# Two boundaries and the output projection of a macaron block: when weights are loaded, how the last statistics are summed, how rows are centred and read back

## The chip, the cores and the metric

One Trainium2 chip, all 8 NeuronCores. Each core computes 1024 of the 8192 rows on its own; no core waits for another. The time is the device time in microseconds of the slowest core. The engines of a core are TensorE (PE), VectorE (DVE), ScalarE (ACT) and GpSimd (POOL); SyncE (SP) issues most DMAs, and POOL issues the stores. Each engine takes its instructions in the order in which they were emitted and waits on semaphores.

## The reference

```
x = x + 0.5 * ffn(layernorm(x))          # FFN 1
x = x + attn(layernorm(x))
x = x + 0.5 * ffn(layernorm(x))          # FFN 2, the same weights

ffn(x):  out = x @ W_base.T + b
         + 2 * sum over the top-2 of 8 experts, gate * B_e @ (A_e @ x), rank 16
attn(x): Q = x @ Wq.T (32 heads of 128), K, V = x @ Wk.T, x @ Wv.T (one head)
         rotary tables on Q and K
         windows of 512 keys every 256 rows, sigmoid(QK/sqrt(128)) / its row sum,
         neighbouring windows blended linearly; then @ Wo.T
layernorm: (x - mean) / sqrt(var + 1e-5), no weights
```

x is [2, 4096, 4096] fp32, the weights 4096 x 4096.

## The kernel before

Everything is transposed: features on the 128 partitions, rows of x along the free axis. A core holds 1024 own rows and 512 of its neighbours for K and V: three tiles t of 512 rows (t = 0 and 1 are its own, 2 the neighbours'). A tile of 4096 features is 32 chunks c of 128 x 512. The centred rows stand in SBUF as bf16 (`xc[t]`). A weight matrix is 32 tiles of 128 outputs, each 2 MB of fp32: two halves are loaded into two staging buffers and cast by ACT to bf16 into one of three slots (`wring`). One group (of, t) is 32 matmuls of 128x128 by 128x512 into one of four PSUM banks; in an FFN a 33rd adds the experts' part (`bpart`).

The stages, in the order in which every engine's program is written out by hand (there is no planner; `pr.emit` and `pr.dma` append to the lists of an engine, and the order of the Python calls is the order in each queue):

1. FFN 1 (lines 485 to 679): rows arrive, are centred, gated, and multiplied; x1 goes to HBM (`x1h`). From of = 3 to 28 the loop is of over t. The last three tiles 29 to 31 are done tile by tile in the order t = 2, 0, 1.
2. First boundary: the layernorm of x1. Its sums are kept by POOL in `acc1` and `acc2` (`evac`, lines 373 to 406), with the square by ACT. `bstats` (606) lets PE add them over the partitions, ACT and DVE make mean and variance. x1 is read back (`x1_load`) chunk by chunk into a ring of nine slots and centred by DVE (`bcenter`, 618). K and V of the three tiles (`kv_mm`, 719) follow chunk by chunk, with rotary tables (`tables`, 689, Sqrt on ACT and a reciprocal on DVE).
3. Attention, 64 slots of a head and half of the rows (lines 786 to 991).
4. Output projection (lines 993 to 1074, and 1103 to 1110): Wo on the heads' outputs, x1 read back and added by DVE (L389), sums by POOL, x2 to HBM (`x2h`).
5. Second boundary and FFN 2 (lines 1076 to 1202): x2 is read back into a ring of sixteen slots, centred, gated by `gating` (304), and multiplied; the first groups follow the centring chunk by chunk (`f2_k` with `chase`).

`wtile` (246) emits both loads and both casts of a weight tile at one place. In stage 4 that place is behind the groups of tile k, for tile k + 2:

```
tok = wo_group(of, t)                  # ends with wo_load(n + 4), an SP read of x1
wt_done[WT[of]]["end"] = tok
WT[of + 2] = wtile(wo_h[of + 2])       # SP: two loads; ACT: two casts
```

An evacuation reads its summand from one of four slots; the read for the fourth group on waits for the store, the add and the square of this one (`xs_free`).

## Time and profile before

| | us |
|---|---|
| median of three timed runs | 2874.55 (2871.07 to 2884.6) |
| the profiled execution | 2889.44 |
| its span on the slowest core (4) | 2887.7 |
| spans of the eight cores | 2854.6 to 2887.7 |
| PE busy | 2486.7 (86%) |
| DVE, ACT, POOL busy | 1095.7, 939.0, 753.9 |
| read from HBM, written | 408.65 MB, 58.72 MB |

A busy PE is not a PE at its peak: the granted clock of a stretch stands beside it. FFN 1 runs steadily from about 360 to 910 us, the first boundary to about 1094, attention to 1804, the output projection to about 2324, the second boundary to about 2480, FFN 2 to the end.

### The profile page before, as it was taken

The page shows a single profiled execution, that of the slowest core. Times are in us where ns is not written, and L with a number is a line of the kernel's source. Part 1 is how long each engine was busy: PE and PEld are TensorE (multiplying, and loading weights), DVE is VectorE, ACT ScalarE, POOL GpSimd, SP SyncE. Part 2 cuts the span into 40 slices and gives each one's busy share as a digit, 9 for nine tenths or more (in the row PEclk, how much of TensorE's full clock was granted, in tenths as well). Part 3 has the DMA queues.
Part 4 walks back from the last instruction along what each step waited for, and adds up shares of the span by engine and source line. Part 5 has one row for each costly group of instructions (what it writes and reads, how often), then busy time and mean ns, then how long its engine had stood idle before and what let it go on. Part 6 is the DMA issues. An engine that isn't in the chain of part 4 may idle for free.

```text
span 2887.7 us, 37498 instructions; the slowest of 8 cores (2854.6 to 2887.7 us)
## 1 busy us (share of the span) xinstructions
PE 2486.7 (86%) x12841; PEld 1198.4 (42%) x13084; DVE 1095.7 (38%) x2668; ACT 939.0 (33%) x1016; POOL 753.9 (26%) x696
## 2 busy tenths in 40 slices
PE   2645799999999868999999999978888788999999
PEld 2434344444443324444444444433333324444444
DVE  2334122211211667888888887100000034211111
ACT  2312122222222124555555554233322322122222
POOL 5645243444343201111111110423333330000000
PEclk9767899999999879999999999988999979999999
DMA  7521254445444883232232322455455575466664
GB/s 248 178 73 59 97 182 162 161 160 179 164 164 179 269 265 111 89 103 93 99 103 89 103 91 101 159 207 191 176 188 199 189 255 207 169 214 218 219 218 179
DMA packets 115307, 469.83 MB, mean 163 GB/s; under 512 B 14768, under 2 KB 15024, under 8 KB 79280
## 3 DMA queue, kind: packets, MB, share of 16 engines
q1 hardware_dynamic: 97200, 408.69, 41.6%
q0 software_dynamic: 17920, 58.73, 5.2%
q8 instruction: 106, 1.74, 0.3%
q14 instruction: 81, 0.66, 0.1%
HBM read 408.65 MB, written 58.72 MB: 162 GB/s over the span
## 4 chain that ended last, share of the span: by engine, by line
PE 40%; DMA 18%; DVE 16%; issue 9%; DVEq 8%; POOL 4%; ACT 3%; SPq 1%; ACTq 0%; POOLq 0%
PE PS L282 36%; DVEq L48 8%; DMA arena<-wo 7%; DMA x2h<-arena 4%; DMA arena<-wb 3%; DVE arena L891 3%; DVE arena L897 3%; POOL arena L439 3%; DMA arena<-x1h 2%; DVE arena L889 1%; DVE arena L893 1%; DVE arena L708 1%; SPq L43 1%; DVE arena L709 1%; DVE arena L621 1%
## 5 line engine op out<-in xcount | busy, mean ns | idle before, releaser
L282 PE MATMUL PS<-arena 128*128 128x512 bf16 x6953 | 1618.5, 390 | 121.3 <-ACT arena L239 106.9
L282 PEld LDWEIGHTS PS<-arena 128*128 128x128 bf16 x7102 | 707.4, 100 | 1004.5 <-issue 259.2
L239 ACT ACTIVATE arena<-arena 128x2048 bf16<-128x2048 f32 (+1 forms) x332 | 517.0, 1577 | 1108.3 <-DMA arena<-wb 644.3
L812 PE MATMUL PS<-arena 128*128 128x512 bf16 x1965 | 545.6, 380 | 4.4
L383 DVE TENSOR_TENSOR arena<-PS,arena 128x512 f32<-128x512 f32 x160 | 110.5, 690 | 890.8 <-PE PS L355 838.8
L854 ACT ACTIVATE arena<-PS 128x512 bf16<-128x512 f32 x384 | 229.0, 597 | 315.2 <-PE PS L851 312.0
L400 POOL TENSOR_TENSOR arena<-arena 128x512 f32<-128x512 f32 x160 | 207.4, 1296 | 429.6 <-ACT arena L398 424.6
L713 POOL TENSOR_TENSOR arena<-arena 128x512 bf16<-128x512 f32 x64 | 80.9, 1264 | 682.6 <-DVE arena L887 601.0
L812 PEld LDWEIGHTS PS<-arena 128*128 128x128 bf16 x2048 | 188.2, 98 | 138.6 <-issue 6.1
L389 DVE TENSOR_TENSOR arena<-PS,arena 128x512 f32<-128x512 f32 x64 | 44.1, 690 | 483.2 <-PE PS L282 478.0
L399 POOL TENSOR_TENSOR arena<-arena 128x512 f32<-128x512 f32 x160 | 215.7, 1348 | 3.4
L398 ACT ACTIVATE arena<-arena 128x512 f32<-128x512 f32 x160 | 95.5, 620 | 328.9 <-DVE arena L386 299.0
L870 PE MATMUL PS<-arena 128*128 128x130 bf16 x1536 | 130.7, 220 | 38.8 <-DVE arena L887 16.2
L43 POOL DMA_DIRECT2D out<-arena x64 | 34.6, 541 | 474.3 <-DVE arena L386 416.6
L870 PEld LDWEIGHTS PS<-arena 128*128 128x128 bf16 x1536 | 97.0, 97 | 142.7 <-issue 127.1
L851 PE MATMUL PS<-arena 128*128 128x512 bf16 (+1 forms) x512 | 145.7, 325 | 0.7
L386 DVE SCALAR_TENSOR_TENSOR arena<-arena 128x512 f32<-128x512 f32 x160 | 140.4, 878 | 15.5 <-issue 0.9
L43 POOL DMA_DIRECT2D x1h<-arena x96 | 53.7, 559 | 353.4 <-DVE arena L386 329.3
L621 DVE TENSOR_TENSOR arena<-arena 128x512 bf16<-128x512 f32 x160 | 113.3, 774 | 26.6 <-DMA arena<-x1h 23.5
L439 POOL TENSOR_TENSOR arena<-arena 128x512 f32<-128x512 f32 x72 | 115.1, 1598 | 11.0 <-POOL arena L439 0.9
L897 DVE SCALAR_TENSOR_TENSOR arena<-PS,arena 128x128 f32<-128x128 f32 x256 | 89.7, 350 | 24.9 <-issue 1.9
L891 DVE TENSOR_TENSOR arena<-arena 128x2 f32<-128x2 f32 x256 | 89.5, 350 | 25.1 <-issue 2.2
(95 smaller groups left out, 1237.2 us busy)
## 6 DMA issues: line engine op xcount, KB each, us to landing
arena<-wb SPq DMA_DIRECT2D x128, 1024.0 KB, 7.4
arena<-wq SPq DMA_DIRECT2D x64, 1024.0 KB, 5.0
arena<-wo SPq DMA_DIRECT2D x64, 1024.0 KB, 6.6
arena<-x1h SPq DMA_DIRECT2D x160, 256.0 KB, 5.1
arena<-x2h SPq DMA_DIRECT2D x128, 256.0 KB, 4.9
arena<-xp SPq DMA_DIRECT2D x12, 2048.0 KB, 11.8
arena<-xr SPq DMA_DIRECT2D x96, 256.0 KB, 2.7
x1h<-arena POOLq DMA_DIRECT2D x96, 256.0 KB, 2.4
```

Of the source, the lines that this page charges most:

```text
L48: self.ops[e].append((lambda v: v.drain(), (), None, 0))
L239: a.activation(d, s, ACT.Copy), [g, extra] if j == 0 else [])
L282: tok = pr.emit(PE, lambda t, c=c, b=b, w=w, n=n, fin=fin, r=rhs_t: t.matmul(bank(b), w[:, c, :], r[:, c, :], start=(n == 0), stop=(fin an ...
L399: p = pr.emit(POOL, lambda q: q.tensor_tensor(a1, a1, xs, ALU.add), [ev, acc_tok.get((f is f2, t))])
L400: q2 = pr.emit(POOL, lambda q: q.tensor_tensor(a2, a2, s, ALU.add), [sq])
L439: tok = pr.emit(POOL, lambda q, k=k: q.tensor_tensor(f_hs, f_hs, x[:, k * 512:(k + 1) * 512], ALU.add), [tok])
L812: tok = pr.emit(PE, lambda q, c=c: q.matmul(bank(b), w[:, c, :], xc[hf][:, c, :], start=(c == 0), stop=(c == NC - 1)), ws, c == NC - 1)
L851: tok = pr.emit(PE, lambda q, s=s, q0=q0, nq=nq, i=i: q.matmul(bank(b)[:, i * nq:(i + 1) * nq], krb[:, s * 128:(s + 1) * 128], qrb[u % 2][ ...
L854: sb_free[b] = sc_ev[(u, k)] = pr.emit(ACE, lambda a: a.activation(sgb[u % 2][:, k * 512:(k + 1) * 512], bank(b), ACT.Sigmoid, scale=SCALE ...
L870: tok = pr.emit(PE, lambda q, i=i, sl=sl, o=o: q.matmul(bank(b)[:, (i // 2) * 130:(i // 2) * 130 + 130], sgb[u % 2][:, o:o + 128], vext[:, ...
L891: pr.emit(DVE, lambda v: v.tensor_tensor(sm[:, 4:6], sm[:, 2:4], a01[:, 2 * Q:2 * Q + 2], ALU.mult))
L897: pr.emit(DVE, lambda v: v.scalar_tensor_tensor(t2, U[:, 130:258], sm[:, 6:7], t1, ALU.mult, ALU.add))
```

## The change

- **Loads and casts are separate.** `wload` issues the loads of a tile, `wcast` the two casts, which wait for the slot of the tile three before. In the steady loops tile of + 2 is cast at the start of tile of, and tile of + 3 is loaded right behind it.
- **Last statistics.** For the groups 29 to 31 of a row tile, ACT writes a bf16 copy and a bf16 square, and PE adds them over the partitions (`stat_mm`) at chunk 18 of a following group (10 and 18 for the last), on top of two fp32 matmuls over what POOL has summed up to tile 28. `stat_end` makes the mean and variance; the mean stays in PSUM.
- **Centring in pairs** of chunks, 128 x 1024: DVE reads the mean from PSUM, every fourth pair is POOL's, with the mean in SBUF.
- **Reads back.** Eight pairs of x1 are read at tile 25 of FFN 1 and the ring has eight slots (four at the end); twelve pairs of x2 are read at tile 26 of the projection, and eight more at the end of group (31, 0).
- **K and V of tile 2** use PSUM banks 0 and 1, and the order of the K/V block is changed. The tables use Ln and Exp on ACT.
- **Gating** is cut in three, which FFN 2 places apart: `rcolumn` (the four fp32 transposes of the row factor and their copy), `gating` (DVE and the sigmoids), `gtrans` (four transposes and a copy). An FFN evacuation writes its product back to PSUM and frees the bank after its second instruction.

The diff, cut to its core:

```diff
-    ring = [ring_r.again().f32(4608)[:, k * 512:(k + 1) * 512] for k in range(9)]
+    ring4 = [ring_r.again().f32(4096)[:, k * 1024:(k + 1) * 1024] for k in range(4)]
+    ring4 += [KVR.again().f32(4096)[:, k * 1024:(k + 1) * 1024] for k in range(4)]
...
-    def stage(src, dst, extra=None, parts=1):
+    stg_q = []
+
+    def load_half(src, dst, tile=None, hf=0):
+
         k = stg_n[0] % 2
         stg_n[0] += 1
-        g = pr.dma(SP, "stg%d" % k, stg[k], src, [stg_free[k]])
+        assert all(q[0] != k for q in stg_q)
+        stg_q.append((k, pr.dma(SP, "stg%d" % k, stg[k], src, [stg_free[k]]), dst, tile, hf))
+
+    def cast_half(extra=None, parts=1):
+        k, g, dst, tile, hf = stg_q.pop(0)
+        ws = [g, extra]
+        if tile is not None and tile >= 3 and hf == 0:
+            free = wt_done[tile - 3].get("end")
+            assert free is not None, tile
+            ws.append(free)
         s3 = resh(stg[k], (16, 128))
+        n = 16 // parts
         c = None
         for j in range(parts):
-            n = 16 // parts
             c = pr.emit(ACE, lambda a, d=dst[:, j * n:(j + 1) * n, :], s=s3[:, j * n:(j + 1) * n, :]:
-                        a.activation(d, s, ACT.Copy), [g, extra] if j == 0 else [])
+                        a.activation(d, s, ACT.Copy), ws if j == 0 else [])
         stg_free[k] = c
+        if tile is not None:
+            wt_done[tile]["tok"][hf] = c
         return c
...
-    def wtile(src, parts=1, half=None, k=None):
...
+    def wload(src, half=None, k=None):
...
         w = wring[k % 3]
-        free = wt_done[k - 3].get("end") if k >= 3 else None
-        if k >= 3:
-            assert free is not None, k
         for hf in ((0, 1) if half is None else (half,)):
-            wt_done[k]["tok"][hf] = stage(src[:, hf * 2048:(hf + 1) * 2048],
-                                          w[:, hf * 16:(hf + 1) * 16, :],
-                                          free if hf == 0 else None, parts)
+            load_half(src[:, hf * 2048:(hf + 1) * 2048], w[:, hf * 16:(hf + 1) * 16, :], k, hf)
+        return k
...
+    def wcast():
+
+        cast_half()
+        cast_half()
+
+    def wtile(src, parts=1, half=None, k=None):
+        k = wload(src, half, k)
+        for _ in ((0, 1) if half is None else (half,)):
+            cast_half(None, parts)
...
         if kind == "ffn":
-            tm = f["tmp"][j]
-            e = pr.emit(DVE, lambda v: v.tensor_tensor(
-                tm, bank(b), f["rh"][:, t * 512:(t + 1) * 512], ALU.mult), [mm, xs_ld[n]])
+            pr.emit(DVE, lambda v: v.tensor_tensor(
+                bank(b), bank(b), f["rh"][:, t * 512:(t + 1) * 512], ALU.mult), [mm, xs_ld[n]])
             pr.drain()
             ev = pr.emit(DVE, lambda v: v.scalar_tensor_tensor(
-                xs, tm, bh[:, of:of + 1], xs, ALU.add, ALU.add))
+                xs, bank(b), bh[:, of:of + 1], xs, ALU.add, ALU.add))
         else:
-            e = ev = pr.emit(DVE, lambda v: v.tensor_tensor(xs, bank(b), xs, ALU.add), [mm, xs_ld[n]])
-        bank_free[b] = e
+            ev = pr.emit(DVE, lambda v: v.tensor_tensor(xs, bank(b), xs, ALU.add), [mm, xs_ld[n]])
+        bank_free[b] = ev
         st = pr.dma(POOL, "st%d" % k, dst, xs, [ev])
         st_tok[(kind, of, t)] = st
         free = [st]
-        if stat:
+        s = f["sqs"][j]
+        if stat == "late":
+            sb = s.bitcast(BF16)
+            pr.emit(ACE, lambda a: a.activation(sb[:, 0:512], xs, ACT.Copy), [ev, sqs_free[j]])
+            sq = pr.emit(ACE, lambda a: a.activation(sb[:, 512:1024], xs, ACT.Square))
+            late.setdefault((kind, t), []).append((sb, sq, j))
+            free.append(sq)
+        elif stat:
             a1 = f["acc1"][:, t * 512:(t + 1) * 512]
             a2 = f["acc2"][:, t * 512:(t + 1) * 512]
-            s = f["sqs"][j]
             sq = pr.emit(ACE, lambda a: a.activation(s, xs, ACT.Square), [ev, sqs_free[j]])
-            p = pr.emit(POOL, lambda q: q.tensor_tensor(a1, a1, xs, ALU.add), [ev, acc_tok.get((f is f2, t))])
+            p = pr.emit(POOL, lambda q: q.tensor_tensor(a1, a1, xs, ALU.add), [ev, acc_tok.get((kind, t))])
             q2 = pr.emit(POOL, lambda q: q.tensor_tensor(a2, a2, s, ALU.add), [sq])
-            acc_tok[(f is f2, t)] = q2
+            acc_tok[(kind, t)] = q2
             sqs_free[j] = q2
-            acc_tok[t] = q2
             free += [p, sq]
         xs_free[k] = free
         return ev
+
+    late = {}
...
+    def stat_mm(f, kind, t, n, bm_, bs_, ws=()):
+
+        if n == 0:
+            for src, b in ((f["acc1"], bm_), (f["acc2"], bs_)):
+                pr.emit(PE, lambda q, b=b, s_=src[:, t * 512:(t + 1) * 512]: q.matmul(
+                    bank(b), onesf, s_, start=True, stop=False), [acc_tok[(kind, t)]] + list(ws), False)
+        sb, sq, j = late[(kind, t)][n]
+        pr.emit(PE, lambda q: q.matmul(bank(bm_), onesb, sb[:, 0:512], start=False, stop=(n == 2)), [sq], False)
+        tok = pr.emit(PE, lambda q: q.matmul(bank(bs_), onesb, sb[:, 512:1024], start=False, stop=(n == 2)))
+        sqs_free[j] = tok
+        return tok
+
+    def stat_end(f, t, bm_, bs_, tok):
+
+        a1 = f["acc1"][:, t * 512:(t + 1) * 512]
+        a2 = f["acc2"][:, t * 512:(t + 1) * 512]
+        pr.emit(ACE, lambda a: a.activation(a1, bank(bm_), ACT.Copy), [tok])
+        m = pr.emit(ACE, lambda a: a.activation(a2, bank(bm_), ACT.Square))
+        v = pr.emit(DVE, lambda v: v.tensor_tensor(a2, bank(bs_), a2, ALU.subtract), [m])
+        return m, v
 
 
...
+    def pair_load(key, src, t, c, slot, slot_key, waits):
+        rg_ld[key] = pr.dma(SP, "rg%s" % slot_key, slot, src[t, c:c + 2].rearrange("c p n -> p c n"),
+                            [rg_free.get(slot_key)] + list(waits))
+
+    def pair_center(f, key, t, c, slot, slot_key, dst, bm_, m_tok, pe_tok, eng):
+        o = dst[:, c:c + 2, :]
+        if eng == DVE:
+            mean = bank(bm_)
+        else:
+            mean = f["acc1"][:, t * 512:(t + 1) * 512]
+        rg_free[slot_key] = pr.emit(eng, lambda v: v.tensor_tensor(
+            o, slot, mean.unsqueeze(1).broadcast_to([128, 2, 512]), ALU.subtract),
+            [rg_ld[key], m_tok, pe_tok])
+        return rg_free[slot_key]
...
+    def x1_center(k):
+        for _ in range(k):
+            n = x1_done[0]
             t, c = x1_seq[n]
-            ctr2[(t, c)] = bcenter(f1, t, c, n, ring, xc[t], bm[t], xdone[t])
-            x1_load(1)
-
-    for t in (2,):
-        for of in range(29, 32):
+            sk, sl = x1_slot(n)
+            ctr2[(t, c)] = ctr2[(t, c + 1)] = pair_center(
+                f1, n, t, c, sl, sk, xc[t], MB[t][0], bm[t], xdone[t], POOL if n % 4 == 3 else DVE)
+            x1_done[0] += 1
+            while x1_n[0] < len(x1_seq) and x1_n[0] - (8 if x1_n[0] < 36 else 4) <= n:
+                x1_load(1)
...
+    W[3] = wtile(wb_h[3])
+    W[4] = wtile(wb_h[4])
+    W[5] = wload(wb_h[5])
+    for of in range(3, 29):
+        wcast()
+        if of + 3 < 32:
+            W[of + 3] = wload(wb_h[of + 3])
+        for t in range(3):
             tok = f1_k(of, t)
...
+    wcast()
+    Wk = wload(wk_h)
+    g, tok, mm = f1_last(29, 2)
+    f1_lev(29, 2, g, mm)
+    g, tok, mm = f1_last(30, 2, at(18, lambda: f1_late(2, 0, stat_ws)))
+    f1_lev(30, 2, g, mm)
+    g, tok, mm = f1_last(31, 2, at(18, lambda: f1_late(2, 1)))
+    f1_lev(31, 2, g, mm)
+    xdone[2] = tok
+
+    g, tok, mm = f1_last(29, 0, at(18, lambda: f1_late(2, 2)))
+    stat_done(2, box["tok"])
+    x1_center(2)
+    f1_lev(29, 0, g, mm)
+    g, tok, mm = f1_last(30, 0, at(18, lambda: f1_late(0, 0, stat_ws)))
+    x1_center(5)
+    f1_lev(30, 0, g, mm)
+    g, tok, mm = f1_last(31, 0, at(18, lambda: f1_late(0, 1)))
+    x1_center(5)
+    f1_lev(31, 0, g, mm)
...
-    Wk = Wv = None
...
+    g, tok, mm = f1_last(29, 1, at(18, lambda: f1_late(0, 2)))
+    wt_done[W[29]]["end"] = tok
+    x1_center(4)
+    c2_end = [pr.now(DVE)]
+    stat_done(0, box["tok"])
+    f1_lev(29, 1, g, mm)
+    wcast()
+    Wv = wload(wv_h)
+    g, tok, mm = f1_last(30, 1)
+    wt_done[W[30]]["end"] = tok
+    x1_center(5)
+    f1_lev(30, 1, g, mm)
+    wcast()
+    WQ = {0: wload(wq_h[0])}
+    g, tok, mm = f1_last(31, 1, at(18, lambda: f1_late(1, 0, c2_end)))
+    wt_done[W[31]]["end"] = tok
+    x1_center(5)
+    f1_lev(31, 1, g, mm)
+    wcast()
...
-        r2_tok[t] = pr.emit(DVE, lambda v: v.reciprocal(a2, a2), [s])
-        pr.drain()
+        ln = pr.emit(ACE, lambda a: a.activation(a2, a2, ACT.Ln, bias=eps1, scale=1.0), [bv[t]])
+        r2_tok[t] = pr.emit(ACE, lambda a: a.activation(a2, a2, ACT.Exp, scale=-0.5), [ln])
         dst = tabh if t == 2 else tab[t]
...
-    kv_mm(2, 0)
-    bm[1], bv[1] = bstats(f1, 1)
+    WQ[1] = wload(wq_h[1])
...
+    kv_mm(2, 0, late1)
+    late_end = box["tok"]
+    x1_center(3)
+    stat_done(1, late_end)
     tb2 = tables(2, 0)
-    x1_center(64, 74)
+    x1_center(3)
+    ctr0_end = pr.now(DVE)
+    kvr_ws = [rg_free[k] for k in range(4, 8)]
+    kv_mm(2, 1)
     k_evac(2, tb2)
-    kv_mm(2, 1)
+    bank_free[0] = kv_free[0]
+    x1_center(4)
+    kv_mm(0, 0)
     v_evac(2)
+    bank_free[1] = kv_free[1]
+    x1_center(3)
     tb0 = tables(0, 1)
-    x1_center(74, 85)
-    kv_mm(0, 0)
+    kv_mm(0, 1)
     v_trans(2)
     k_evac(0, tb0)
-    kv_mm(0, 1)
+    x1_center(4)
     v_evac(0)
-    x1_center(85, 96)
+    x1_center(5)
...
+    wcast()
+    WT[3] = wload(wo_h[3])
...
+            pair_load(n, x2h, t, c, sl, "x%d" % sk, [st_tok[("wo", c, t)], st_tok[("wo", c + 1, t)]] +
+                      (att_ws if n < 12 else [o0_done]))
...
+            if n >= 8:
+                ws += [rg_free["x%d" % k] for k in range(4)]
+            if n >= 16:
+                ws += [rg_free["x%d" % k] for k in range(4, 12)]
+            eng = POOL if n % 4 == 3 else DVE
+            o = xc3[t][:, c:c + 2, :]
+            mean = bank(MB2[t][0]) if eng == DVE else f2["acc1"][:, t * 512:(t + 1) * 512]
+            ctr3[(t, c)] = ctr3[(t, c + 1)] = rg_free["x%d" % sk] = pr.emit(
+                eng, lambda v, o=o, sl=sl, mean=mean: v.tensor_tensor(
+                    o, sl, mean.unsqueeze(1).broadcast_to([128, 2, 512]), ALU.subtract),
+                [rg_ld[n], bm2[t]] + ws)
+            x2_done[0] += 1
+            while 20 <= x2_n[0] < len(x2_seq) and x2_n[0] - 8 <= n:
+                x2_load(1)
...
+        if of > 1:
+            wcast()
+            if of not in (4, 5):
+                if of + 3 < 32:
+                    WT[of + 3] = wload(wo_h[of + 3])
+        if of == 4:
...
+            load_half(wa_h[:, 0:2048], f2["ar"][:, 0:16, 0:128])
+            load_half(wa_h[:, 2048:4096], f2["ar"][:, 16:32, 0:128])
...
+            if of in (4, 5) and t == 0:
+                cast_half()
+                bb2_tok = cast_half()
+                WT[of + 3] = wload(wo_h[of + 3])
+        if of == 4:
+            ar2_tok = bb2_tok
+        if of == 26:
+            x2_load(12)
         wt_done[WT[of]]["end"] = tok
-        if of + 2 < 32:
-            WT[of + 2] = wtile(wo_h[of + 2])
...
+    g, mm = wo_last(29, 0)
+    wo_lev(29, 0, g, mm)
+    g, mm = wo_last(30, 0, at(18, lambda: f2_late(0, 0, b2_ws)))
+    wo_lev(30, 0, g, mm)
+    g, mm = wo_last(31, 0, at(18, lambda: f2_late(0, 1)))
+    wo_lev(31, 0, g, mm)
+    o0_done = mm
+    x2_load(8)
+
+    g, mm = wo_last(29, 1, at(18, lambda: f2_late(0, 2)))
+    wt_done[WT[29]]["end"] = mm
+    stat2_done(0, box["tok"])
+    x2_center(3)
+    wo_lev(29, 1, g, mm)
+    wcast()
+    WF[1] = wload(wb_h[1])
+    g, mm = wo_last(30, 1, at(18, lambda: f2_late(1, 0, b2_ws)))
+    wt_done[WT[30]]["end"] = mm
+    x2_center(5)
+    wo_lev(30, 1, g, mm)
+    wcast()
+    WF[2] = wload(wb_h[2])
+    g, mm = wo_last(31, 1, at(18, lambda: f2_late(1, 1)))
+    wt_done[WT[31]]["end"] = mm
+    x2_center(5)
+    wo_lev(31, 1, g, mm)
+    wcast()
+    WF[3] = wload(wb_h[3])
...
+        ln = pr.emit(ACE, lambda a: a.activation(rh, a2, ACT.Ln, bias=eps4, scale=4.0), [bv2[t]])
+        rh_tok[t] = pr.emit(ACE, lambda a: a.activation(rh, rh, ACT.Exp, scale=-0.5), [ln])
+        return rh_tok[t]
...
-    f2_k(0, 0, True)
-    bm2[1], bv2[1] = bstats(f2, 1)
-    rchain2(0)
-    x2_center(32, 42)
+    f2_k(0, 0, True, at(18, lambda: f2_late(1, 2)))
+    stat2_done(1, box["tok"])
+    r0 = rchain2(0)
+    x2_center(3)
+    ar_free[0], ar_free[1] = bv2[0], bv2[1]
+    for p in range(4):
+        at_ = aphase_piece(f2, xc3[0], p, [ar2_tok])
     f2_k(1, 0)
-    for p in range(4):
-        at = aphase_piece(f2, xc3[0], p, [ar2_tok])
-    hw2[0] = None
-    x2_center(42, 50)
+    rc2 = rcolumn(f2, 0, r0, None)
+    b6_free[0] = rc2
+    g2 = gating(f2, 0, at_, rc2)
+    x2_center(6)
     f2_k(2, 0)
-    hw2[0] = gating(f2, 0, at, rchain_tok[0], b6_free[0])
-    b6_free[0] = pr.now(ACE)
-    rchain2(1)
-    x2_center(50, 64)
+    hw2[0] = gtrans(f2, 0, g2)
+    r1 = rchain2(1)
+    x2_center(7)
     wt_done[WF[0]]["end"] = f2_k(0, 1, True)
-    WF[3] = wtile(wb_h[3])
+    wcast()
+    WF[4] = wload(wb_h[4])
     for _ in range(3):
         f2_b()
+    for p in range(4):
+        at_ = aphase_piece(f2, xc3[1], p, [])
+    rc2 = rcolumn(f2, 1, r1, b6_free[0])
+    g2 = gating(f2, 1, at_, rc2)
     wt_done[WF[1]]["end"] = f2_k(1, 1)
-    WF[4] = wtile(wb_h[4])
-    for p in range(4):
-        at = aphase_piece(f2, xc3[1], p, [])
+    wcast()
+    WF[5] = wload(wb_h[5])
     wt_done[WF[2]]["end"] = f2_k(2, 1)
-    hw2[1] = gating(f2, 1, at, rchain_tok[1], b6_free[0])
-    first3 = f2_k(3, 0)
+    hw2[1] = gtrans(f2, 1, g2)
+    f2_k(3, 0)
     pend2.insert(0, pend2.pop())
-    f2_b()
...
     for of in range(3, 32):
+        if of > 3:
+            if of + 2 < 32:
+                wcast()
+            if of + 3 < 32:
+                WF[of + 3] = wload(wb_h[of + 3])
```

## Rows read from the trace of the kernel before

**Rows 1.** Waits of PE over the span: total us, times, longest.
```profile
PE PS L282 <- ACT arena L239: 106.9, 30, 20.7
PE PS L610 <- POOL arena L400: 26.5, 2, 15.1
PE PS L757 <- DVE arena L748: 18.9, 2, 9.6
PE PS L1151 <- DVE arena L621: 17.0, 23, 5.1
```

**Rows 2.** Busy time by stretch: PE, PEld, DVE, ACT, POOL, clock, DMA, GB/s.
```profile
1804.30:2323.90 519.60, 440.22 (x1856) 190.96 (x1891) 42.89 (x62) 154.50 (x126) 182.51 (x180) 0.92 0.52 186
2480.00:2882.00 402.00, 395.20 (x1790) 178.02 (x1825) 79.33 (x110) 103.15 (x54) 29.93 (x56) 1.00 0.61 213
909.80:1094.40 184.60, 131.92 (x537) 57.38 (x547) 111.09 (x148) 37.57 (x34) 31.94 (x31) 0.84 0.77 255
2323.90:2480.00 156.10, 123.46 (x662) 59.18 (x670) 69.58 (x118) 32.36 (x32) 22.25 (x20) 0.85 0.64 213
```

**Rows 3.** Timeline of DVE in the output projection: start, us, instruction [idle before].
```profile
2161.70 0.69 DVE L389 TENSOR_TENSOR arena<-PS,arena 128x512 f32<-128x512 f32 x1 [6.88 <-PE PS L282]
2168.61 0.69 DVE L389 TENSOR_TENSOR arena<-PS,arena 128x512 f32<-128x512 f32 x1 [6.21 <-PE PS L282]
```

**Rows 4.** Waits of the SP queue in the output projection.
```profile
SPq L1216 <- DMA x2h<-arena: 269.8, 51, 21.2
SPq L1216 <- ACT arena L398: 161.2, 28, 9.9
```

**Rows 5.** Timeline of all engines in the output projection.
```profile
2057.74 5.72 SPq L43 DMA_DIRECT2D arena<-x1h  x2
...
2063.51 0.92 SPq L43 DMA_DIRECT2D arena<-wo  x2
...
2068.91 1.91 ACT L239 ACTIVATE arena<-arena 128x2048 bf16<-128x2048 f32 x1 [10.73 <-DMA arena<-wo]
...
2071.08 14.17 PE L282 MATMUL PS<-arena 128*128 128x512 bf16 x57 [2.83 <-ACT arena L239]
```

**Rows 6.** DMA issues of the page: KB each, median us to landing.
```profile
arena<-wb SPq DMA_DIRECT2D x128, 1024.0 KB, 7.4
```

**Rows 7.** Busy time by stretch, first boundary.
```profile
990.00:1000.00 10.00, 9.91 (x39) 4.17 (x39) 6.14 (x10) 2.78 (x2) 0.56 (x1) 0.82 1.00 346
...
1020.00:1030.00 10.00, 5.79 (x11) 2.15 (x12) 7.62 (x9) 1.13 (x2) 3.51 (x3) 0.52 0.99 319
```

**Rows 8.** Busy time of FFN 1, of core 0 and then of core 4.
```profile
400.00:900.00 500.00, 494.18 (x2290) 223.85 (x2288) 101.02 (x140) 129.63 (x116) 216.13 (x210) 1.00 0.49 174
400.00:900.00 500.00, 497.09 (x2190) 222.63 (x2233) 101.45 (x136) 123.29 (x112) 208.77 (x203) 0.96 0.46 167
```

**Rows 9.** Timeline of PE at the first boundary.
```profile
910.04 7.07 PE L282 MATMUL PS<-arena 128*128 128x512 bf16 x31
...
946.91 1.02 PE L610 MATMUL PS<-arena 128*128 128x512 f32 x2
...
948.63 7.07 PE L282 MATMUL PS<-arena 128*128 128x512 bf16 x32
...
981.60 2.04 PE L610 MATMUL PS<-arena 128*128 128x512 f32 x2 [11.44 <-POOL arena L400]
...
1024.21 2.04 PE L610 MATMUL PS<-arena 128*128 128x512 f32 x2 [15.07 <-POOL arena L400]
```

**Rows 10.** Instructions of two lines: duration in ns, min/median/max.
```profile
L459 DVE TENSOR_TENSOR arena<-arena x12: 4410/4426/5492, 42.3 to 265.2; 128x4096 bf16<-128x4096 f32 x12
L399 POOL TENSOR_TENSOR arena<-arena x160: 1272/1277/6627, 162.5 to 2368.0; 128x512 f32<-128x512 f32 x160
```

**Rows 11.** Timeline of PE: second boundary (A phase), and the end.
```profile
2351.69 2.28 PE L1151 MATMUL PS<-arena 128*128 128x512 bf16 x4 [5.12 <-DVE arena L621]
...
2436.94 7.74 PE L297 MATMUL PS<-arena 128*128 128x136 bf16 x128
...
2881.87 0.38 PE L355 MATMUL PS<-arena 128*128 128x512 bf16 x1
```

264 lines of the change are left out of this document (124 added, 140 removed).

## The prediction, made before the changed kernel was run

> **What bounds the kernel now.** I read in this order: who waited for whom over the whole span, the busy time by stage, then the timeline of each stage that loses time. TensorE (PE) is the bound, and its work doesn't change much, so the question is where it stands still and where it runs at the lower clock. In the list of waits five eighths of what this change can reach is one line: 106.9 us, in 30 waits, for the cast of a weight tile (L282 on L239); then come 26.5 us for the statistics' adds (L610 on POOL's L400), 18.9 us for the V evacuation and 17.0 us for centring [rows 1]. By stage, PE was busy 440.2 of 519.6 us in the output projection (D, to the end of group (31,0)), 131.9 of 184.6 us at the first boundary (B, from the start of group (29,2) to the second Q group), 123.5 of 156.1 us at the second (E), at granted clocks of 0.92, 0.84 and 0.85; in the steady second FFN it is 395.2 of 402.0 us at 1.00 [rows 2]. Attention and the first 900 us are not touched in any way that PE sees.
>
> The price of full speed: two evacuations in D lie 6.91 us apart, that is 32 matmuls of 0.216 us [rows 3]. A group of 33 in an FFN costs 7.13 us.
>
> **Why D waits.** SP issues in order. The read of x1 for the evacuation four groups on waits for the store that frees its slot (SP waited 269.8 us for stores and 161.2 us for the squares) [rows 4], and the weights of tile k+2 are queued behind it. In the timeline the two reads hold SP from 2057.74 to 2063.46, the weights go out at 2063.51, the cast can start at 2068.91, and PE goes on at 2071.08 after 2.83 us [rows 5]. The cast at the head of ACT's queue also holds back the squares, so POOL's adds and the next store, which feeds the first delay.
>
> **D, part by part.** After: tile k+3 is loaded once tile k+2 is cast, and cast one tile later. The load leaves SP some 5.5 us into a tile (same SP delay), lands 7.4 us later (median of the wb loads [rows 6]), at 13 to 15; its cast is due at 13.8 + 1.5, and PE wants it 12 us after that. So the waits of 75 us in this window and the slow matmuls behind them go. Sum: 59 groups x 6.91 = 407.7; last head 0.4; statistics of tile 0, two fp32 matmuls as now 1.7 and four bf16 ones 0.9 (the last two lie in E); 410.7 in all, against 519.6. Added: twelve reads of 0.5 MB after tile 26, 6.3 MB. At the 319 GB/s of a full DMA [rows 7] they take 20 us and stand ahead of tile 30's weights; the slack is about 27 us, so 0 to 8, I take 4. The staging of A and B at tiles 4 and 5 delays a load by a tile at most, out of two tiles of slack: 0 to 4, I take 0. Clock: a dense FFN 1 ran at 1.00 on core 0 and 0.96 on core 4 for 500 us [rows 8]; on 411 us this is 0 to 17, I take 6. D = 421, saves **99** (bounds 80 to 109).
>
> **B.** Now: 910.04 to 1094.38. PE stands from 970.16 to 981.60 and from 1009.14 to 1024.21 because the square and adds of the last group come late, behind casts and eleven centrings; the chases behind crawl [rows 9]. After, at full speed: 521 matmuls of 0.216 = 112.5; three statistics of 1.72 (bank 6 and 7 fp32 matmuls, 946.91 to 948.63 [rows 9]) + 6 x 0.216 = 9.1; transposes 1: 122.6. It can't be reached, for two reasons.
> (1) DMA. Only 8 of 48 pairs are preloaded. From the first centring, which needs the mean of tile 2 at chunk 18 of (29,0), 31.5 us into B, 40 pairs (21.0 MB), three weight tiles (6.3 MB) and some 3.2 MB of reads, stores and tables must pass: 30.5 MB at 319 GB/s = 96 us, so the last pair lands at about 127, where PE at full speed would need it at 114. After it: its centring 1, the rest of kv_mm(1,0) about 1, kv_mm(1,1) 6.9.
> (2) The end of B stays serial on VectorE (DVE): tables, rope, V evacuation, transposes. The reciprocal on DVE goes, the ACT pair that replaces it is behind the cast of WQ[1]: I take 6 of the wait, now 18.9 - 9.6 = 9.3 [rows 1] (bounds 2 to 10).
> Sum 127 + 2 + 6.9 + 6 = 142; restarts at half clock 2: 144, saves **40** (bounds 15 to 58; full DMA reached 346 in one stretch [rows 7], and the in-order ACT may cost more: the cast of WQ[0] stands ahead of stat_done(1)).
> Centring: a DVE pair is 1024 elements. 4096 took 4.41 us [rows 10], so 1.08 ns each and about 1.17 us for a pair with its start. Pairing itself gives next to nothing, since the cost goes with the elements; the fourth pair on POOL does: 1.28 us for 512 [rows 10], so 2.5. Bounds for the DVE pair with a PSUM mean, which the trace doesn't show: 1.1 to 1.4 (a PSUM and an SBUF input took 0.69 for 512, isolated [rows 3]). None of it is on the path while DMA is.
>
> **E.** Now: 2323.9 to the last matmul at 2882.25 [rows 11], 558.4. Full speed: three groups 20.7, statistics 3.5, 64 FFN groups x 33 x 0.216 = 456.2, two A phases x 7.7 [rows 11], gating on PE 3: 498.9. Loss now 59.4, of which the two crawling chases, two gatings (PE waits for L339) and the evacuation behind them. After, with T the start of (29,1): the mean of tile 0 is there at T+6; DVE does 12 pairs and three evacuations, POOL four; pair 15 is ready at about T+26 where PE wants it at T+30. No wait. For tile 1 ACT must first cast WF[2], which lands at T+30, so the mean comes at T+33, not T+29; pairs 16 to 18 follow, then DVE is held by the gating until T+51 and the rest is done at T+64 where the chase begun at T+54 would end at T+61: 4 lost. The burst of four evacuations holds bank 3: 2.6 (now 1.8), as an evacuation keeps its bank for both of its instructions, 1.5 us in place of 0.7. In the steady FFN this is hidden by four banks of 7.1 us each. DMA 2, clock 3. E = 510.5, saves **48** (bounds 30 to 58).
>
> The rest: Ln and Exp in place of Sqrt and reciprocal are beside PE; FFN 1's evacuation through PSUM is hidden (DVE was busy 79.3 of 402.0 us in a steady FFN [rows 2]); the 20.7 us wait for W[3], the longest of its line [rows 1], stays, because SP still reaches W[3] after the same reads: 0. W[5] is now cast ahead of the squares of the first groups: POOL gets late by some 10 us and has 20.
>
> Total 99 + 40 + 48 = 187. The profiled execution took 2889.4 us with its span of 2887.7, above all the three timed runs (median 2874.55): core 4's 0.96 in FFN 1 is about 20 us of it, which no edit touches. So I take 187 off the median: **2687.5**.
>
> **A rule weighed.** POOL's add beside DVE's back-to-back centrings took up to 6.63 us, 1.28 otherwise [rows 10]. The Trainium skill (page "SBUF — State Buffer", section on the engine and DMA sides) says that a DVE instruction with two SBUF inputs takes a port pair that GpSimd shares and keeps it to its end; with the mean in PSUM there is one SBUF input, and by that rule POOL's pair stays at 2.5. No row shows POOL beside a run of centrings with a PSUM mean, so this is open until the profile after.
>
> **Rivals.**
> (a) The boundaries give little: DMA is full for B, ACT's casts stand before both second means. B saves 15, E 25, D 99: 2874.5 - 139 = **2736**. For: DMA share 0.99 at 1020 [rows 7]; against: E's volume fits.
> (b) Dense work lowers the clock. D and E get 0.96 as core 4 did: 0.04 x 909 = 36, less the 9 that I have: 2687 + 27 = **2714**. Against: the second FFN at 1.00 with PE 98% busy. The Trainium skill (page "TensorE: Matmul & The Clock Gate", section "Seeing it yourself") says more: a peak-current limiter takes a die with three densely working cores to 13/16. By that the 909 us would become 1119 and the gain would be gone (about 2897); rows 2 and 8 show 402 and 500 us of dense work without it, on a die whose cores all work.
> (c) Slower than before: POOL's pairs. 20 of the 80 pairs go to POOL, and each is waited for in order by DVE's slots and by PE. If DVE starves POOL as it does now, a pair costs up to 2 x 6.63 = 13.3, 265 in all on the path: 2687 + 265 = **2952**. It decides from 187/20 = 9.4 us a pair. Against: the rule above, and that a starved POOL holds only 12 + 8 spots.
> (d) The change doesn't do what it says in D: not the order of SP but DMA volume is the limit (3.1 MB per 13.8 us = 227 GB/s, in bursts). Then D saves 50: **2737**. Against: the steady FFN moves 213 GB/s at a share of 0.61 without waits [rows 2].
>
> **How the numbers follow.** Forecast 0.62 (own range 2662 to 2712), (a) 0.18, (b) 0.08, (d) 0.08, (c) and the limiter together 0.03, something within half a per cent of no change 0.01. Half a per cent (14 us) is what this measurement tells from none. The range takes in (a), (b) and (d) and the low bound of all three parts (109 + 58 + 58 = 225 gives 2650): 2655 to 2748. Faster 0.96, same 0.01, slower 0.03.
>
> **What would show it.** D: waits of L282 for the cast near 0, PE about 99% busy, evacuations 6.9 apart throughout. B: DMA share near 1 from the first centring to kv_mm(1,0), PE waits only there and before the V transposes, 144 long. E: no wait before the first FFN group, a few us in the chase of tile 1. POOL's pairs at 2.5 us. Wrong if the D waits stay with loads landing late, if the clock of dense stretches is under 0.95 on most cores, or if B is longer than 170.

## The result, and the profile after

2713.4 us (median of 4 runs, 2710.7 to 2725.3) against 2879.6 for the kernel before, measured beside it (4 runs, 2871.1 to 2889.8): a ratio of 0.943, 95% interval 0.938 to 0.948. It is 6% faster; 166 us went, where 187 were forecast. The forecast was 2687.5; 2713.4 lies just above its own range (2662 to 2712) and inside the whole range (2655 to 2748). In some executions of every kernel the cores of one die show a lower granted clock and the time is some per cent longer; the ratios and times below leave those out. The profiled execution took 2725.3 us (span 2723.4), 164.1 less than the one before (2889.4).

Stages of the profiled executions, slowest core, in us (in brackets the median over the eight cores):

| stage | before | after | saved | forecast |
|---|---|---|---|---|
| A, to the start of group (29,2) | 910.0 (891.9) | 898.6 (882.6) | 11.4 (9.3) | 0 |
| B, first boundary | 184.3 (183.8) | 177.1 (173.8) | 7.2 (10.0) | 40 |
| C, attention | 709.9 (710.2) | 711.2 (711.0) | -1.3 (-0.8) | 0 |
| D, projection to (31,0) | 519.6 (513.8) | 421.4 (420.2) | 98.2 (93.6) | 99 |
| E, to the last matmul | 558.3 (558.8) | 509.6 (511.5) | 48.7 (47.3) | 48 |

D and E came as forecast. B gave a fifth to a quarter of its forecast, and A gave 9 to 11 us that I had put at nothing. The total is nearer to its forecast than B is only because A, by luck, paid back a third of what B lacked.

Waits of PE over the span, after (total, times, longest), to be laid beside [rows 1]:

```profile
PE PS L831 <- DVE arena L657: 26.9, 4, 13.8
PE PS L306 <- ACT arena L251: 23.7, 2, 22.0
...
PE PS L450 <- ACT arena L426: 16.0, 3, 9.3
```

The 106.9 us for the cast of a weight tile are 23.7, and 22.0 of them are W[3]'s in FFN 1, which the prediction left standing. The adds' 26.5 us became 16.0 for the copies and squares that PE now sums (L450 on L426). The line at the top is centring in the K/V block (L657), for which PE did not wait in the kernel before.

The windows that answer to [rows 2], in the order B, D, E, steady FFN (length, busy time of PE, PEld, DVE, ACT, POOL, granted clock, DMA share, GB/s):

```profile
898.60:1075.67 177.07, 131.51 (x553) 56.36 (x563) 76.00 (x85) 39.79 (x44) 36.46 (x24) 0.86 0.68 218
1786.80:2208.20 421.40, 411.47 (x1863) 186.41 (x1900) 43.11 (x62) 152.10 (x126) 178.19 (x176) 0.99 0.71 247
2208.20:2717.90 509.70, 498.13 (x2456) 235.12 (x2500) 128.43 (x186) 137.68 (x92) 55.10 (x75) 1.00 0.62 217
2300.00:2700.00 400.00, 395.37 (x1808) 180.05 (x1843) 83.82 (x116) 103.08 (x55) 31.34 (x58) 1.00 0.61 215
```

D went from a clock of 0.92 to 0.99. In B the DMA share *fell*, from 0.77 to 0.68, where I had it near 1.

**D after.** One tile of the timeline of all engines, against [rows 5]:

```profile
2057.75 32.54 PE L306 MATMUL PS<-arena 128*128 128x512 bf16 x147
...
2065.08 3.69 ACT L251 ACTIVATE arena<-arena 128x2048 bf16<-128x2048 f32 x2
...
2066.65 1.54 SPq L43 DMA_DIRECT2D arena<-x1h  x2
...
2068.28 0.90 SPq L43 DMA_DIRECT2D arena<-wo  x2
...
2078.89 3.69 ACT L251 ACTIVATE arena<-arena 128x2048 bf16<-128x2048 f32 x2
```

The weights asked for at 2068.28 are cast at 2078.89 without a wait, and a tile takes 13.81 us (2065.08 to 2078.89), 64 matmuls at full speed.

**B after.** Timelines of PE, of DVE, and of SP's queue:

```profile
984.88 0.58 PE L450 MATMUL PS<-arena 128*128 128x512 bf16 x1 [9.27 <-ACT arena L426]
...
1016.47 9.98 PE L831 MATMUL PS<-arena 128*128 128x512 bf16 x37 [13.77 <-DVE arena L657]
...
1047.32 4.13 PE L831 MATMUL PS<-arena 128*128 128x512 bf16 x8 [10.29 <-DVE arena L657]
```

```profile
979.46 2.53 DVE L657 TENSOR_TENSOR arena<-arena,PS 128x1024 bf16<-128x1024 f32 x2 [8.65 <-DMA arena<-x1h]
981.90 0.69 DVE L411 TENSOR_TENSOR PS<-PS,arena 128x512 f32<-128x512 f32 x1
...
1012.66 1.68 DVE L800 TENSOR_TENSOR arena<-arena 128x512 f32<-128x512 f32 x1 [15.46 <-DMA arena<-sinx]
...
1055.92 1.22 DVE L657 TENSOR_TENSOR arena<-arena,PS 128x1024 bf16<-128x1024 f32 x1 [0.80 <-DMA arena<-x1h]
```

```profile
991.98 3.87 SPq L43 DMA_DIRECT2D arena<-wq  x2
...
998.02 0.70 SPq L43 DMA_DIRECT2D arena<-sinx  x1
1021.48 10.70 SPq L43 DMA_DIRECT2D arena<-x1h  x7
```

These rows form a circle. The rotary tables (cos, sin) are asked for behind 2 MB of Q weights; DVE stands 15.46 us for them, with centrings behind it whose data are there; a centring that isn't done frees no slot, so SP asks for no x1 from 997 to 1021.48; and the DMAs then run dry. Windows of after (DMA share and GB/s at the end of the row):

```profile
1000.00:1010.00 10.00, 2.70 (x13) 1.02 (x11) 0.00 (x0) 0.49 (x1) 0.87 (x1) 0.79 1.00 344
1010.00:1020.00 10.00, 3.42 (x9) 1.06 (x10) 7.03 (x8) 0.00 (x0) 2.34 (x1) 0.53 0.13 49
...
1040.00:1050.00 10.00, 2.45 (x6) 0.45 (x7) 9.68 (x12) 0.00 (x0) 2.59 (x1) 0.50 0.07 10
```

**E after.** The longest waits of PE from 2208 on:

```profile
PE PS L306 <- DVE arena L414: 2.7, 1, 2.7
PE PS L321 <- DVE arena L461: 2.5, 1, 2.5
PE PS L1335 <- POOL arena L1203: 1.8, 1, 1.8
PE PS L1335 <- DVE arena L1203: 1.6, 3, 0.7
```

### The profile page after: what moved, and what is told of

Read it like the earlier page. It is cut to its first block, busy times and chain, and to the rows that moved or that the text cites. A ratio compares the mean times of both kernels' runs of the same rounds, so it can differ in the third digit from the quotient of the medians.

```text
span 2723.4 us, 37240 instructions; the slowest of 8 cores (2698.8 to 2723.4 us)
## 1 busy us (share of the span) xinstructions
PE 2436.5 (89%) x12871; PEld 1191.4 (44%) x13114; DVE 1024.1 (38%) x2563; ACT 946.4 (35%) x1036; POOL 755.4 (28%) x686
## 4 chain that ended last, share of the span: by engine, by line
PE 57%; DVE 15%; DVEq 8%; DMA 6%; issue 6%; POOL 3%; ACT 2%; SPq 1%; another core or an unknown queue 0%; POOLq 0%; ACTq 0%
PE PS L306 53%; DVEq L48 8%; DVE arena L1008 3%; DVE arena L1014 3%; POOL arena L495 2%; DVE arena L1006 2%; DMA arena<-wb 2%; DVE arena L809 2%; DVE arena L1010 1%; DVE arena L810 1%; PE PS L384 1%; DMA arena<-wo 1%; SPq L43 1%; ACT arena L523 1%; DMA arena<-sinx 1%
## 5 line engine op out<-in xcount | busy, mean ns | idle before, releaser
L306 PE MATMUL PS<-arena 128*128 128x512 bf16 x6956 | 1579.1, 384 | 35.5 <-ACT arena L251 23.7
L251 ACT ACTIVATE arena<-arena 128x2048 bf16<-128x2048 f32 (+1 forms) x332 | 510.1, 1572 | 508.5 <-PE PS L306 229.6
L929 PE MATMUL PS<-arena 128*128 128x512 bf16 x1964 | 545.3, 380 | 3.3
L411 DVE TENSOR_TENSOR PS<-PS,arena 128x512 f32<-128x512 f32 x160 | 111.8, 699 | 892.6 <-PE PS L384 828.7
L434 POOL TENSOR_TENSOR arena<-arena 128x512 f32<-128x512 f32 x145 | 184.5, 1273 | 50.8 <-ACT arena L432 50.8
L433 POOL TENSOR_TENSOR arena<-arena 128x512 f32<-128x512 f32 x145 | 192.7, 1329 | 3.1
L417 DVE TENSOR_TENSOR arena<-PS,arena 128x512 f32<-128x512 f32 x64 | 44.2, 691 | 383.4 <-PE PS L306 351.7
L968 PE MATMUL PS<-arena 128*128 128x512 bf16 x511 | 145.5, 326 | 1.9
L414 DVE SCALAR_TENSOR_TENSOR arena<-PS,arena 128x512 f32<-128x512 f32 x160 | 120.1, 750 | 15.6 <-issue 0.9
L495 POOL TENSOR_TENSOR arena<-arena 128x512 f32<-128x512 f32 x72 | 114.5, 1591 | 11.0 <-POOL arena L495 0.9
L43 POOL DMA_DIRECT2D x2h<-arena x64 | 35.7, 557 | 233.0 <-DVE arena L417 232.9
## 6 DMA issues: line engine op xcount, KB each, us to landing
arena<-x1h SPq DMA_DIRECT2D x48, 512.0 KB, 8.6
```

Source lines behind the costliest of these rows:

```text
L43: self.ops[e].append((lambda q, o=out, i=in_: q.dma_start(out=o, in_=i), tuple(t for t in waits if t is not None), sem, 16))
L251: a.activation(d, s, ACT.Copy), ws if j == 0 else [])
L306: tok = pr.emit(PE, lambda t, c=c, b=b, w=w, n=n, fin=fin, r=rhs_t: t.matmul(bank(b), w[:, c, :], r[:, c, :], start=(n == 0), stop=(fin an ...
L433: p = pr.emit(POOL, lambda q: q.tensor_tensor(a1, a1, xs, ALU.add), [ev, acc_tok.get((kind, t))])
L434: q2 = pr.emit(POOL, lambda q: q.tensor_tensor(a2, a2, s, ALU.add), [sq])
L495: tok = pr.emit(POOL, lambda q, k=k: q.tensor_tensor(f_hs, f_hs, x[:, k * 512:(k + 1) * 512], ALU.add), [tok])
```

## The experiments

Ratios are to the kernel before, measured beside each. Stage lengths are medians over the eight cores of the profiled run, against the brackets in the table above; kernels are named after what they change.

**a_old_place**: the kernel after, with the projection's weights where they were.

```diff
-        if of > 1:
-            wcast()
-            if of not in (4, 5):
-                if of + 3 < 32:
-                    WT[of + 3] = wload(wo_h[of + 3])
...
         wt_done[WT[of]]["end"] = tok
+        WT[of + 2] = wtile(wo_h[of + 2])
```

> The changed kernel with one part undone: the weight tiles of the output projection are loaded and cast at the old place, behind the groups of tile k for tile k+2. Theory 1 (the place of the loads in SP's queue made the waits, and moving it gave the 98 us of D): D goes back from 421 to about 515 us, PE waits for casts of about 75 us come back, the whole is 2713 + 94 = about 2805. Rival (the gain in D came from elsewhere, e.g. from the staging of A and B or the early reads): D stays under 450 and the whole under 2745.

Ratio 0.986 (0.977 to 0.996), 2839.2 and 2840.5 us where 2805 were expected; D 534.2 (after: 420.2; expected 515), B 172.7, E 510.2. PE waits 111.8 us for the cast, as before. The weights' edit is the whole gain of D. That D is 20 us longer than before's 513.8 comes from the twelve early reads of x2, which this kernel keeps: SP asks for them at 2232.97, ahead of two reads of the next weights, and here nothing is loaded ahead to cover it. ACT's cast waits, and PE then stands 19.3 us at 2260.64, where before has no wait over 11.0 in D.

```profile
2258.48 1.91 ACT L251 ACTIVATE arena<-arena 128x2048 bf16<-128x2048 f32 x1 [30.84 <-DMA arena<-wo]
```

**b_head**: the kernel before, with load and cast of tile k+2 at the head of tile k.

```diff
+        if of > 1:
+            WT[of + 2] = wtile(wo_h[of + 2])
         tok = None
...
-        if of + 2 < 32:
-            WT[of + 2] = wtile(wo_h[of + 2])
```

> The kernel before with one thing moved: the loads and casts of weight tile k+2 of the projection are emitted ahead of the groups of tile k instead of behind them. No third tile ahead. Theory 1 (place in SP's queue): the loads leave some 14 us earlier, D falls from 520 to 420 to 440 us and the whole from about 2878 to 2790. Rival (two tiles ahead are not enough, since a cast at the head of ACT's queue waits for its load and holds the squares, the adds, the stores and so SP): half the waits stay, D about 470, the whole about 2830.

Ratio 0.995 (0.993 to 0.997); D 501.6, 12 of after's 94 us, and longer than either theory had (420 to 440, or 470). A place one tile further forward in SP's queue, which the prediction named first, is worth little. The timeline of all engines shows why:

```profile
2070.23 5.76 SPq L43 DMA_DIRECT2D arena<-x1h  x2
...
2076.04 0.94 SPq L43 DMA_DIRECT2D arena<-wo  x2
...
2081.20 1.91 ACT L239 ACTIVATE arena<-arena 128x2048 bf16<-128x2048 f32 x1 [10.52 <-DMA arena<-wo]
...
2083.89 1.91 ACT L239 ACTIVATE arena<-arena 128x2048 bf16<-128x2048 f32 x1 [0.78 <-DMA arena<-wo]
2085.70 1.13 ACT L398 ACTIVATE arena<-arena 128x512 f32<-128x512 f32 x2
2086.39 5.83 SPq L43 DMA_DIRECT2D arena<-x1h  x2
```

A closed loop of 16.16 us (2070.23 to 2086.39) against the 13.8 that PE needs: two reads (5.8), weights asked for, landed and cast by 2085.80 (9.8), the square that had waited at the cast's back (0.57), and only then is the slot free for the next read.

**l_no_sums**: the kernel before; the sums of x2 and of its squares are left out in the projection, so nothing stands behind a cast.

```diff
-        evac(f2, "wo", of, t, g, mm, x2h[t, of])
+        evac(f2, "wo", of, t, g, mm, x2h[t, of], stat=False)
```

> The kernel before with the sums of x2 left out in the output projection (no square on ACT, no two adds on POOL), the weights at their old place. Theory 4 (a closed loop through ACT: a cast waits for its load at the head of ACT's queue, the squares wait behind it, the adds and the next store behind them, SP's reads behind those, the next weights behind the reads; one turn takes 16 us where two groups take 13.8): with the squares gone the loop is open, D falls from 520 to 420 to 435, PE's waits for casts from 75 to under 10 us. Theory 1 as first put (the weights are simply issued too late, behind the reads of their own tile): store 4 + reads 6 + landing 7 + cast 2 = 19 us from the last evacuation is still over 13.8, D stays above 480.

Ratio 0.970 (0.966 to 0.974); D 434.1 (expected 420 to 435), 80 us shorter with the weights at their old place. Opening the loop is enough. What is left to 420 are waits for the cast of 22.5 us in 15 on one core, more than the 10 expected. The edit takes the squares and POOL's adds out together, so it doesn't say which of them weighs more; in b_head's rows it is the square that lets the next read go.

**q_cast_now**: the kernel after; in tiles 9 to 27 the weights are asked for directly ahead of their cast, not a tile earlier.

```diff
-        if of > 1:
+        if 9 <= of <= 27:
+            WT[of + 2] = wload(wo_h[of + 2])
             wcast()
...
+        elif of > 1:
+            wcast()
```

> The kernel after, with one thing changed in 19 tiles of the output projection (9 to 27): the tile's weights are asked for directly ahead of their cast (both at the head of the tile two ahead of their use), where the change asks for them a whole tile before the cast. Theory (the cast and the squares share ScalarE, so a cast whose transfer is under way holds the squares, the squares hold the adds, the adds the store and the buffer, and these the next reads): the 19 tiles go at a period of 15.5 to 16.5 us where the kernel after has 13.9 to 14.1, so the projection stage is 30 to 45 us longer (451 to 465 for 420.2), and the whole 2740 to 2758. Rival (what counts is only that the reads are issued at the head of the tile): the stage stays within 5 us of 420, the whole within 0.2% of the kernel after.

Ratio 0.962 (0.959 to 0.965); D 470.5. From tile to tile SP's weight reads lie 16.4 us apart (1882.41 to 2161.31 in 17 steps), the upper end of what I expected. D is longer than the 451 to 465 expected, since at the hand-over behind tile 27 one more wait of 21.7 us came up: as in a_old_place, the twelve early reads of x2 (2176.61) stand ahead of the next weights, and no tile is loaded ahead to cover it. With b_head and l_no_sums this settles D: what counts is that the transfer lies *between* the request and the cast, in time in which ACT works.

**c_halfread**: the kernel after; of each x1 pair at the first boundary only one half is read, and used twice.

```diff
-            pair_load(n, x1h, t, c, sl, sk, [st_tok[("ffn", c, t)], st_tok[("ffn", c + 1, t)]] + rg_ws)
+            rg_ld[n] = pr.dma(SP, "rg%s" % sk, sl[:, 0, :], x1h[t, c],
+                              [rg_free.get(sk), st_tok[("ffn", c, t)], st_tok[("ffn", c + 1, t)]] + rg_ws)
```

> The changed kernel with half of x1's read back left out at the first boundary: each pair reads only its first chunk, which is centred twice, so 12.6 MB of 25.2 MB go. All instructions and their order stay. B was 177 us where 144 was forecast. Theory 2 (volume: DMA full is what B waits for): B falls by up to 10.5 MB / 319 GB/s = 33 us, to about 145. Theory 3 (order: DVE stands at the tables' multiplications for cos and sin, which are queued behind the Q weights, and no x1 read is issued meanwhile): the wait before the tables shrinks only as far as the queue ahead of cos and sin does, the gaps with an idle DMA stay, and B falls by 15 us at most, to 162 or more.

Ratio 0.938 (0.932 to 0.944); B 150.9, 23 less, between the two theories (145, and 162 or more). So volume counts; but a third less of it leaves B still above the 144 forecast with all of it. It isn't volume alone either: the shorter queue ahead of the tables cuts DVE's two waits for sin from 15.46 and 7.96 us to 9.61 and 5.39.

**d_wq1_late**: the kernel after, Q's second weight tile asked for behind the second pair of tables.

```diff
-    WQ[1] = wload(wq_h[1])
...
     tb0 = tables(0, 1)
+    WQ[1] = wload(wq_h[1])
```

> The changed kernel with the load of the second Q weight tile (2.1 MB) issued behind the loads of cos and sin of both tables instead of ahead of them. Theory 3 (order): cos and sin land 6 to 7 us earlier, DVE's wait at the first tables falls from 15.5 to about 9 and that at the second from 8 to about 8 (nothing was moved there), B about 168, whole about 2705. Theory 2 (volume): the same bytes still pass before the last pair, so B stays at 174 to 178 and the wait only moves.

Ratio 0.943 (0.934 to 0.953), the same as after's: the whole time, expected at 2705, doesn't show it (median 2716.1, 2701.2 to 2730.9). The stage does: B 165.5, 8 less for one moved line, with every byte still ahead of the last reads of x1, and DVE's first wait for sin is 8.40 us (expected 9).

**e_order**: the kernel after, the whole first boundary reordered: both pairs of tables are asked for ahead of the K/V block, Q's weights behind its first centrings, and centrings go ahead of tables and K evacuation.

```diff
+    tload(2, 0)
+    tload(0, 1)
...
     stat_done(1, late_end)
+    WQ = {0: wload(wq_h[0])}
...
+    x1_center(4)
     tb2 = tables(2, 0)
...
     tb0 = tables(0, 1)
+    wcast()
+    WQ[1] = wload(wq_h[1])
```

> The changed kernel with the first boundary reordered: cos and sin of two tables are issued ahead of both Q weight tiles; the first Q tile is loaded at the start of the K/V block and cast behind the tables' Ln and Exp, the second is loaded behind that cast; on DVE the evacuation of (31,1) stands ahead of the last two of its five centrings, and the first tables' multiplications stand behind four more centrings. The halved read took 27 us off B and the later load of one tile 12, so both volume and order count. If it is the order of the queues (theory 3): the 9.3 us wait for the late copy, the 15.5 us wait for sin and the idle DMA at 1010 and 1040 go, B falls from 177 to 140 to 150, whole about 2685. If volume alone (theory 2): DMA passes the same 30 MB from the first centring to the last pair, but moves 4 MB of it behind the last x1 pair, so at most 13 us: B 164, as with the one tile moved.

2692.8 us (2692.1 to 2699.6), ratio 0.934 (0.930 to 0.938); B 155.6, 18 less, which again lies between the theories (140 to 150, and 164; their 27 and 12 us are of the slowest core). Two windows, 119 to 139 us into B (after's 0.13 lies at 111 to 121):

```profile
1000.00:1010.00 10.00, 5.54 (x20) 1.55 (x18) 7.63 (x11) 0.00 (x0) 0.00 (x0) 0.82 0.99 293
1010.00:1020.00 10.00, 3.73 (x8) 0.84 (x8) 3.73 (x4) 0.00 (x0) 3.17 (x2) 0.50 0.83 294
```

The DMAs no longer run dry before the last pair is in, and its centring begins 134.9 us into B (DVE, 1016.3) where after has 157.3 (1055.92). Contrary to theory 2, both Q tiles are still asked for ahead of the last reads of x1 (997.37 and 999.73): from the first centring to that one the core moved 289 GB/s over 104.4 us at a share of 0.91, 30.2 MB. The bytes are the same; the rate rose.

**r_best**: e_order, with the casts behind the copies and squares that PE waits for, at both boundaries.

```diff
     f1_lev(31, 1, g, mm)
+    wcast()
...
     wo_lev(29, 0, g, mm)
+    wcast()
+    WF = {0: wload(wb_h[0])}
...
     r0 = rchain2(0)
+    wcast()
+    WF[3] = wload(wb_h[3])
```

> The kernel of e_order (first boundary reordered, 2692.8), with the casts on ScalarE put behind the copies and squares that TensorE waits for, at both boundaries: the second half of the V weights behind the late copy of (31,1), the last projection weights behind (29,0)'s, the third FFN tile's behind (31,1)'s, and that of the fourth behind the statistics. In e_order TensorE waits 5.7 us, 8.1 us (two times) and 4.0 us for ScalarE at these places (core 0). Theory: they go, and 2/3 of them isn't lost again to the transfers behind: first boundary 151 to 154 (155.6 before), last stage 502 to 507 (512.0), projection within 3 of 421.9: whole 2678 to 2688. Rival (these waits only stand in for transfers that arrive too late, so that the wait moves to a centring or to weights): within 0.15% of e_order's 2692.8.

Profiled at 2677.8 us, the shortest execution of all; median 2684.8 (2677.8 to 2706.6), ratio 0.936 (0.932 to 0.940), which overlaps e_order's: that it beats e_order isn't settled by the times. By stage it does: B 154.2 (e_order 155.6), D 412.1 (421.9), E 509.9 (512.0). The gain isn't where it was expected: E was to be 502 to 507, and D within 3 us of 421.9. What is left in B, waits of PE from 860 to 1060:

```profile
PE PS L867 <- DVE arena L858: 13.0, 2, 7.2
PE PS L838 <- POOL arena L657: 10.5, 3, 6.2
```

**i_no_early_x2**: the kernel after, the twelve early pairs of x2 asked for with the others behind (31,0).

```diff
-        if of == 26:
-            x2_load(12)
...
-    x2_load(8)
+    x2_load(20)
```

> The kernel after, with the first 12 pairs of the second boundary's read-back asked for behind group (31,0) with the next 8, in place of behind tile 26. Theory: in the projection nothing is gained (the DMAs have room, within 1.5 us), and at the boundary the 12 pairs (6.3 MB at some 320 GB/s, 20 us) come one after the other in front of TensorE's chase, which the last three groups (21 us) cover only in part: the last stage is 12 to 25 us longer (524 to 537 for 511.5), whole 2725 to 2738. Rival (the chase is paced by the centrings on VectorE, 38 pairs in 45 us, not by the transfers): the last stage stays within 4 us of 511.5.

Ratio 0.946 (0.943 to 0.948). E 527.0, 15.5 longer, the size expected but not for the reason: the chase waits 3.1 us in all (after 3.4), and the loss is one wait for the copies behind a cast.

```profile
2225.99 0.58 PE L450 MATMUL PS<-arena 128*128 128x512 bf16 x1 [17.91 <-ACT arena L426]
```

The FFN's weights are now asked for behind twenty pairs of x2 (SP, from 2177.27; the weights at 2204.49), ACT's cast stands 21.54 us for them, and the copy stands behind the cast: the knot of D once more. And D is 410.3, 10 *shorter*, which neither theory had. Reading x2 early is worth some 6 us, not 16: it holds up the last projection weights, and the copies that stand behind their cast (L450 on L426, 6.2 us in after's D, not there here).

**g_all_dve** and **h_mean_sbuf**: the kernel after, with all 80 pairs on DVE; and with DVE's pairs reading the mean from SBUF (the `if False` leaves the copy for both engines).

```diff
-            eng = POOL if n % 4 == 3 else DVE
+            eng = DVE
```

```diff
-        if eng == DVE:
+        if False:
             mean = bank(bm_)
...
-            mean = bank(MB2[t][0]) if eng == DVE else f2["acc1"][:, t * 512:(t + 1) * 512]
+            mean = f2["acc1"][:, t * 512:(t + 1) * 512]
```

> The changed kernel with all 80 pairs centred by DVE, none by POOL. DVE gets 12 + 8 more pairs of 1.2 us. At the first boundary DMA is what centring waits for, so B stays within 4 us of 177. At the second, tile 1 has four more DVE pairs between the gating and the chase: E from 510 to 515, at most 518. Whole 2713 to 2722. Rival (POOL's pairs of 2.35 us are late and hold the slots and PE, 1.8 us at the end of the chase): E falls by 2 to 4, whole 2710.

> The changed kernel with DVE's pairs reading the mean from SBUF, as before the change, instead of from PSUM; the fourth pair stays POOL's. By the rule that a DVE instruction with two SBUF inputs locks out POOL, POOL's pairs and stores beside DVE's runs take up to 6 us instead of 2.35, and those chained behind them wait: B 177 to 190, E 510 to 520, whole 2713 to 2735. Rival (no row of this kernel depends on it, since POOL gets its turn between two pairs): POOL's pair stays under 3.5 us, B and E within 2 us, whole 2713.

Ratios 0.943 (0.936 to 0.949) and 0.942 (0.938 to 0.947): no difference to after for either. B 175.6 and 175.4, E 512.7 and 514.8 (after 173.8, 511.5). The share of POOL earns nothing that can be measured. The mean in PSUM earns nothing in the whole time and some 3 us in E, where the variants that leave this part alone lie between 510.2 and 512.0: with the mean in SBUF, PE's wait for the statistics is 4.8 us (after 2.5) and those in the chase 4.3 (3.4). The mechanism expected was the wrong way round: POOL's pairs took at most 3.2 us, DVE's up to 5.8 (see the last section).

**n_evac_sbuf**: the kernel after, FFN evacuation through a temporary in SBUF, as before.

```diff
-                bank(b), bank(b), f["rh"][:, t * 512:(t + 1) * 512], ALU.mult), [mm, xs_ld[n]])
...
+                tm, bank(b), f["rh"][:, t * 512:(t + 1) * 512], ALU.mult), [mm, xs_ld[n]])
...
-        bank_free[b] = ev
...
+        bank_free[b] = e
```

> The kernel after, with the FFN evacuation as before: its product goes to a temporary in SBUF and the bank is released after the first instruction. Question: the stage up to group (29,2) became 9 us shorter (891.9 to 882.6, medians over the cores), which I had put at nothing. Theory 1 (the evacuation's form does it: 699 + 750 ns for 878 + 752, and less held up beside GpSimd): this stage is back at 890 to 893, and its 256 evacuations in the two FFNs cost nothing elsewhere; the second FFN and its entry loses its wait of 2.7 for a bank and stays within 3 us. Whole 2720 to 2724. Rival (what is loaded and in which order at the start does it, or it is scatter between runs): the stage stays at 881 to 884.

A 889.4 (after 882.6, before 891.9; the nine other variants of after lie between 879.5 and 883.5), the rest as after (2720.9 and 2722.7 us; two executions are too few for a ratio). So the evacuation's form is some 7 of the 9 us. Groups by form, 130 to 290 us, first this kernel, then after (busy, mean ns):

```profile
L415 DVE SCALAR_TENSOR_TENSOR arena<-arena 128x512 f32<-128x512 f32 x6 | 15.6, 2593 | 0.6
```

```profile
L414 DVE SCALAR_TENSOR_TENSOR arena<-PS,arena 128x512 f32<-128x512 f32 x6 | 4.5, 751 | 0.6
```

The same instruction: 2593 ns on average with both inputs in SBUF, 751 with one in PSUM. Of the six, two took 0.75 us and four 3.46 to 3.64, those beside two adds of POOL's (1.27 us each). The six together hold DVE, and the centring of the next FFN tile behind it, 11 us; PE's wait for that centring (L321) is 14.1 us here and 8.9 in after.

## Why the prediction was right where it was, and wrong where it wasn't

**D: the size right, the reason half wrong.** PE's waits for casts went, a tile took 13.81 us. The prediction's first cause, "SP issues in order" with the weights "queued behind it", is not enough: b_head put the weights a tile further forward and saved 12, l_no_sums left them where they were and saved 80. Its next sentence, that the cast at ACT's head holds the squares, "which feeds the first delay", was most of the matter, and it is a loop, not a sum of delays. Two terms of the sum were off and by luck cancelled: 6 for the clock were 0 (0.99 over D, 1.00 where PE is dense), 4 for the early reads were 10 (i_no_early_x2). Without the two the sum says 410.7; i_no_early_x2 has 410.3 and r_best 412.1.

**B: step (1) failed.** The volume was right: from the first centring at 929.2 (30.6 us into B, forecast 31.5) to the last at 1055.9 the core moved 241 GB/s over 126.7 us, which is 30.5 MB, the number of the forecast. The rate was wrong: 319 GB/s, "DMA near 1", needs somebody to ask for the bytes all the time. The share was 0.76, DVE's last pair was centred 157 us into B and POOL's, the very last, landed at 159, not at 127; these 32 us are the miss of 33. In e_order, the same bytes pass at 289 GB/s. I had read the full windows [rows 7] and left the waits of the askers out: a slot of x1 is freed by a centring, DVE takes its work in order, and two of its stops (9.29 us for statistics behind Q's cast on ACT, 15.46 us for tables behind Q's weights on SP) closed the circle. d_wq1_late and e_order bring 8 and 18 back without a byte less. Step (2) held: the wait before the V transposes was 5.8 (forecast 6), the serial end 16 (1059.8 to 1075.7, forecast 15). By the bound set there, B longer than 170, this part was wrong, and its saving of 7 to 10 lies under its own low bound of 15. That is rival (a)'s number for B, but not its reason, since (a) had the DMAs full; and E didn't follow (a).

**Centring.** DVE's pair: 1.22 us, in a row 1.13 apart (forecast 1.17); POOL's 2.35 (forecast 2.5). Rival (c) had nothing to stand on.

**E held by its terms**: chase of tile 1 3.4 (forecast 4), bank 3 2.7 (2.6). Unforeseen were 2.5 for the statistics behind ACT's cast, and in place of my 2 for the DMA and 3 for the clock next to nothing. r_best takes the 2.5 away.

**A: "hidden" was wrong**, see n_evac_sbuf. I had looked at DVE's share in a steady FFN, where it is hidden; in the start of FFN 1 DVE and POOL both are on the path. Of the 9 us 2 to 3 stay open, which is within the 4 us by which kernels with the same stage A differ (879.5 to 883.5).

**Rivals (b) and (d)** fell. By the number alone (b) would have won: it said 2714, and 2713.4 was measured. The stages tell them apart: (b) puts the 27 us into the clock of D and E, which ran dense at 0.99 and 1.00 on all eight cores and came as forecast; the shortfall is B's. And D moved 247 GB/s at a share of 0.71 without a wait for weights in the steady tiles. The Trainium skill (page "TensorE: Matmul & The Clock Gate", section "Seeing it yourself") has a limiter for a die with three dense cores; here D and E, 930 us, ran densely on all eight cores (D in 418.8 to 421.4) and it didn't show. A granted clock of 0.81, the page's 13/16, does occur in these traces, but elsewhere and not always on a whole die. In after it is on cores 0 and 1 alone, in the start of FFN 1; here core 0 and then core 3, of the same die:

```profile
340.00:385.00 45.00, 44.73 (x170) 18.61 (x171) 7.25 (x10) 12.26 (x10) 15.25 (x15) 0.81 0.64 201
340.00:385.00 45.00, 45.00 (x211) 20.39 (x209) 8.70 (x12) 14.81 (x13) 19.55 (x19) 1.00 0.64 228
```

Some 105 us at this clock are why A is 898.6 on core 0 and 882.6 in the median. Core 4's 0.96 in [rows 8], from which (b) was built, is a mean over short stretches at 0.81 (0.81 from 458 to 462 us). What sets it off no run here shows. The range of the prediction has one slip: it is said to take in the 2650 of the three low bounds, and starts at 2655; nothing hangs on it.

## What to carry to other kernels

Ask for a transfer one work period ahead of the in-order instruction that consumes it; if the two stand together, everything behind that instruction (squares, stores, freed buffers, the next reads) closes a loop, and its length, not any engine's load, is the period. Before you price a stage by its bytes over a full rate, follow who asks for each byte and what frees its buffer: a full window in the profile says nothing of the next one. See also what else is asked for ahead of it: twelve early reads cost the projection 10 us in after, and some 20 where no tile was loaded ahead. And price an evacuation where its engine is on the path, not where it is idle.

## What the runs showed of the hardware that I had not expected

With both inputs in SBUF a DVE instruction can stand still while POOL works, for whole instructions of POOL. In h_mean_sbuf (timeline of DVE and POOL), three pairs took 8.08 us, 4.6 more than the 3.49 of three undisturbed ones, beside two of POOL's of 4.68 together; with the mean in PSUM none of the 24 of that line took over 1.222. The instructions of the line in h_mean_sbuf, then in after (ns, min/median/max):

```profile
2199.65 3.49 DVE L1203 TENSOR_TENSOR arena<-arena 128x1024 bf16<-128x1024 f32 x3
...
2203.65 8.08 DVE L1203 TENSOR_TENSOR arena<-arena 128x1024 bf16<-128x1024 f32 x3
...
2204.82 4.68 POOL L1203 TENSOR_TENSOR arena<-arena 128x1024 bf16<-128x1024 f32 x2
```

```profile
L1203 DVE TENSOR_TENSOR arena<-arena x24: 1207/1214/5818, 2199.6 to 2263.2; 128x1024 bf16<-128x1024 f32 x24
L1203 POOL TENSOR_TENSOR arena<-arena x8: 2347/2360/3208, 2204.8 to 2262.7; 128x1024 bf16<-128x1024 f32 x8
```

```profile
L1203 DVE TENSOR_TENSOR arena<-arena,PS x24: 1209/1214/1222, 2214.9 to 2272.1; 128x1024 bf16<-128x1024 f32 x24
L1203 POOL TENSOR_TENSOR arena<-arena x8: 2342/2363/2376, 2220.1 to 2273.4; 128x1024 bf16<-128x1024 f32 x8
```

The Trainium skill (page "SBUF — State Buffer", section "Who interferes with whom") says that which of the two is blocked goes by who issued first, for the whole instruction. The traces agree on who is blocked, if the issue of a store on POOL is counted. In n_evac_sbuf (timeline of all engines):

```profile
160.06 0.68 POOL L43 DMA_DIRECT2D x1h<-arena  x1 [11.41 <-DVE arena L412]
160.17 3.64 DVE L415 SCALAR_TENSOR_TENSOR arena<-arena 128x512 f32<-128x512 f32 x1
160.76 1.27 POOL L434 TENSOR_TENSOR arena<-arena 128x512 f32<-128x512 f32 x1
161.98 1.27 POOL L435 TENSOR_TENSOR arena<-arena 128x512 f32<-128x512 f32 x1
```

DVE's instruction starts ahead of both adds, but during POOL's store issue, and ends behind both adds. All seven long ones of that line in n_evac_sbuf and all six of L1203 in h_mean_sbuf began while POOL was in an instruction or a store issue; none of the other 18 of L1203 did. On how long, the traces go beyond the page's one instruction: the hold lasts over the other engine's instructions that follow without a gap, here two of POOL's. Before, it was POOL that waited (6.63 us for 1.28, [rows 10]), beside eleven centrings of DVE in a row. I had weighed the rule only for POOL; its larger effect in this change was on DVE's evacuations in stage A.
